# Two transformer-like layers on one core: row maxima of two head pairs joined and turned together, second score product eight slots behind instead of five

## The reference, cut to what matters

```python
xn = _layernorm(x)
q, k, v = split(xn @ qkv_w + qkv_b)          # 32 heads of 16 columns
q, k = _rope(q, cos, sin), _rope(k, cos, sin)
scores = einsum('bhqd,bkhd->bhqk', q, k) / 4 + causal mask
probs = softmax(scores)                       # needs each row's maximum first
ctx = einsum('bhqk,bkhd->bqhd', probs, v) @ out_w + out_b
g = silu(ffn(xn))                             # three products with 1376 hidden columns
x = x + ctx * g
```

## Time and profile before

| | us |
|---|---|
| median of three runs | 704.54 |
| lowest, highest | 700.82, 704.76 |
| profiled execution | 699.1 |
| its span | 697.4 |
| PE busy in the span | 622.3 (89%) |
| DVE, ACT, POOL busy | 395.2, 276.8, 370.6 |
| L932 + L941, both score products, PE busy | 44.7 + 37.4 |
| L918, turns of maxima, PE busy, 128 instructions | 19.2 |
| L1219, copies of turned maxima, ACT busy, 64 instructions | 37.4 |

### The profile page before, as it was taken

The page is one execution under the profiler, slowest core; times in us unless marked ns, Lnnn a source line. Parts: engine busy times, 40 slices in busy tenths (PEclk is TensorE's granted clock), DMA queues, the critical chain, the costliest instruction groups (busy, mean ns, idle before and its releaser), DMA issues. The chain is left out here.

```text
span 697.4 us, 9829 instructions
## 1 busy us (share of the span) xinstructions
PE 622.3 (89%) x3372; PEld 425.3 (61%) x3372; DVE 395.2 (57%) x973; ACT 276.8 (40%) x442; POOL 370.6 (53%) x541
## 2 busy tenths in 40 slices
PE   1987899999999997789999999999799999998992
PEld 1855565666557785555656655778577565756660
DVE  4849868666346581986876652649425151515035
ACT  2624545555534422246455564451212343132331
POOL 4765556544333745756554433449802987424445
PEclk9999999999999999999999999999999999999897
DMA  8486765554412326786484336434200000000003
GB/s 294 144 294 200 219 174 159 169 129 110 120 47 75 91 90 169 245 261 181 130 236 135 92 92 261 164 128 138 97 1 0 1 0 1 1 0 1 0 1 120
DMA packets 59889, 83.24 MB, mean 119 GB/s; under 512 B 17840, under 2 KB 26288, under 8 KB 59840
## 3 DMA queue, kind: packets, MB, share of 16 engines
q1 hardware_dynamic: 56192, 71.35, 34.6%
q10 hardware_dynamic: 3648, 11.27, 4.3%
HBM read 64.78 MB, written 26.99 MB: 132 GB/s over the span
## 5 line engine op out<-in xcount | busy, mean ns | idle before, releaser
L729 POOL TENSOR_TENSOR w_lo<-raw,w_hi 128x512 fp32r<-128x512 f32 x98 | 130.8, 1340 | 85.9 <-ACT w_hi L1250 81.5
L1433 DVE CUSTOM_DVE_ANT_0 score_ps<-score_ps,causal 128x512 f32<-128x512 f32 (+3 forms) x256 | 119.9, 517 | 57.3 <-PE score_ps L932 56.7
L1297 ACT ACTIVATE probs_T<-scoreT_ps 128x1024 f32<-128x1024 f32 (+1 forms) x96 | 84.8, 884 | 79.5 <-PE scoreT_ps L941 78.8
L904 PE MATMUL proj_ps<-xn_hi,w_hi 128*128 128x512 f32 x224 | 100.1, 447 | 4.4 <-POOL w_lo L729 2.4
L906 PE MATMUL proj_ps<-xn_lo,w_hi 128*128 128x512 f32 x224 | 88.6, 395 | 0.0
L905 PE MATMUL proj_ps<-xn_hi,w_lo 128*128 128x512 f32 x224 | 88.3, 394 | 0.0
L727 POOL TENSOR_SCALAR w_hi<-raw 128x512 fp32r<-128x512 f32 x50 | 31.1, 621 | 88.4 <-PE proj_ps L906 74.3
L932 PE MATMUL score_ps<-k_st,q_st 50*128 50x512 f32 (+3 forms) x256 | 44.7, 386 | 18.3 <-DVE row_max L1433 15.3
L904 PEld LDWEIGHTS proj_ps<-xn_hi,w_hi 128*128 128x128 f32 x224 | 42.1, 188 | 29.6 <-issue 12.1
L749 POOL TENSOR_SCALAR_AFFINE_SELECT probs_T<-probs_T 128x256 f32<-128x256 f32 x128 | 50.2, 416 | 17.0 <-ACT probs_T L1297 17.0
L932 PEld LDWEIGHTS score_ps<-k_st,q_st 50*128 50x128 f32 x256 | 21.8, 185 | 59.9 <-issue 30.2
(11 more groups left out here) (310 smaller groups left out, 1366.3 us busy)
## 6 DMA issues: line engine op xcount, KB each, us to landing
raw<-w SPq DMA_DIRECT2D x98, 256.0 KB, 2.7
rows<-rows_hi SPq DMA_DIRECT2D x32, 256.0 KB, 3.4
arranged<-tern SPq DMA_DIRECT2D x96, 85.0 KB
q_st<-rows SPq DMA_DIRECT2D x32, 200.0 KB
k_st<-rows SPq DMA_DIRECT2D x32, 200.0 KB
rows<-rows_lo SPq DMA_DIRECT2D x16, 256.0 KB, 4.0
gate_w<-arranged ACTq DMA_DIRECT2D x4, 704.0 KB, 7.0
up_w<-arranged ACTq DMA_DIRECT2D x4, 704.0 KB, 8.5
```

The lines of the kernel that those rows point to most:

```text
L729: nc.gpsimd.tensor_tensor(w_lo[n % SPLIT][:, :], raw[n % RAW][:, :], F32(w_hi[n % SPLIT][:, :]), ALU.subtract).then_inc(unit_ready, 1)
L904: nc.tensor.matmul(acc, lh, rh, start=first, stop=False)
L1297: nc.scalar.activation(probs_T[gp % 4][:, c:c + 2 * w].rearrange("p (h c) -> p h c", h=2), scoreT_ps[:, :, 0:w], ACT.Exp, scale=0.25).then ...
L1433: m = nc.vector.tensor_tensor_reduce(out=block, in0=block, in1=causal[:, S - w:], scale=1.0, scalar=-3e38, op0=ALU.add, op1=ALU.max, accum ...
```

## The change

The three tasks of both pairs of a group are collected before the maxima are joined: `join_maxima`, `max_turn` and `max_out` run once for a group (in slots 6, 12, ... 48) where they ran once for a pair (in slots 3, 6, ... 48). `max_cols` now holds 98 columns in one buffer, with the pairs at columns 0 and 64 and the heads 32 apart. LAG is 8 instead of 5, so SCORE_SLOTS is 56 instead of 53, and the V products, the turns of contexts and the reads of stacks move with it.

```diff
-LAG = 5
+LAG = 8
...
 def read_in(s):
-    return next((g for g in range(1, GROUPS) if (1 if g == 1 else max(6 * g - 6, unit_slot(K_UNIT[g // 2]) + 6)) == s), None)
+    return next((g for g in range(1, GROUPS) if (1 if g == 1 else max(6 * g - 4, unit_slot(K_UNIT[g // 2]) + 6)) == s), None)
...
 def max_in(s):
-    j = s // 3 - 1
-    return j if s % 3 == 0 and 0 <= j < PAIRS else None
+    g = s // 6 - 1
+    return g if s % 6 == 0 and 0 <= g < GROUPS else None
 
 def pv_in(s):
-    g, kt = divmod(s - 12, 6)
-    return (g, kt) if s >= 12 and g < GROUPS and kt <= NT else None
+    g, kt = divmod(s - 15, 6)
+    return (g, kt) if s >= 15 and g < GROUPS and kt <= NT else None
 
 def ctx_in(s):
-    return (s - 17) // 6 if s >= 17 and (s - 17) % 6 == 0 and (s - 17) // 6 < GROUPS else None
+    return (s - 20) // 6 if s >= 20 and (s - 20) % 6 == 0 and (s - 20) // 6 < GROUPS else None
...
-    max_cols = sb("max_cols", [P, 2, NT, 34], f32r)
+    max_cols = sb("max_cols", [P, NT, 98], f32r)
...
-            def max_turn(b, j):
-                pe.wait_ge(max_ready, PAIRS * b + j + 1)
-                n = use(b, ("max", j))
+            def max_turn(b, g):
+                pe.wait_ge(max_ready, GROUPS * b + g + 1)
+                n = use(b, ("max", g))
                 if TURN_BANK[n][1]:
                     pe.wait_ge(turn_done(n), TURN_BANK[n][1])
                 for qt in range(NT):
-                    m = nc.tensor.transpose(turn_bank(n)[0:34, qt * P:(qt + 1) * P], F32(max_cols[:, j % 2, qt, :]), ident[:, :])
+                    m = nc.tensor.transpose(turn_bank(n)[0:98, qt * P:(qt + 1) * P], F32(max_cols[:, qt, :]), ident[:, :])
...
-                        if x == 0:
-                            pe.wait_ge(*copied(b, ("max", j)))
+                        if x == 0 and j % 2 == 0:
+                            pe.wait_ge(*copied(b, ("max", j // 2)))
...
-                for hh in range(2):
-                    m = nc.scalar.activation(q_st[g % 3][64 * hh:64 * hh + 2, j % 2, :], turn_bank(n)[32 * hh:32 * hh + 2, :], ACT.Copy)
+                for p in range(2):
+                    for hh in range(2):
+                        r = 64 * p + 32 * hh
+                        m = nc.scalar.activation(q_st[(GROUPS * b + g) % 3][64 * hh:64 * hh + 2, p, :], turn_bank(n)[r:r + 2, :], ACT.Copy)
                 m.then_inc(turn_done(n), 1)
...
-                        if s % 3 == 2:
-                            join_maxima(b, s // 3)
+                        if s % 6 == 5:
+                            join_maxima(b, s // 6)
```

More of the change, by code:

```diff
@@ L323, in program @@
     causal = sb("causal", [P, S], f32)
-    row_max = sb("row_max", [P, 2, 8], f32)
+    row_max = sb("row_max", [P, 2, NT, 4], f32)
     stat = sb("stat", [P, NT, 6], f32)
@@ L797, in _ @@
                     if b == 0 and u == 1:
-                        nc.gpsimd.memset(F32(max_cols[:, :, :, :]), 0.0).then_inc(cols_set, 1)
+                        nc.gpsimd.memset(F32(max_cols[:, :, :]), 0.0).then_inc(cols_set, 1)
                 if b:
@@ L1212, in copy_out, with max_out @@
                 return nc.scalar.activation(dst, turn_bank(n)[:, :], ACT.Copy)
-            def max_out(b, j):
-                n, g = use(b, ("max", j)), GROUPS * b + j // 2
+            def max_out(b, g):
+                n = use(b, ("max", g))
                 act.wait_ge(turned, n + 1)
-                for hh in range(2):
-                    m = nc.scalar.activation(q_st[g % 3][64 * hh:64 * hh + 2, j % 2, :], turn_bank(n)[32 * hh:32 * hh + 2, :], ACT.Copy)
+                for p in range(2):
+                    for hh in range(2):
+                        r = 64 * p + 32 * hh
+                        m = nc.scalar.activation(q_st[(GROUPS * b + g) % 3][64 * hh:64 * hh + 2, p, :], turn_bank(n)[r:r + 2, :], ACT.Copy)
                 m.then_inc(turn_done(n), 1)
@@ L1433, in row_maxima, with join_maxima @@
                         m = nc.vector.tensor_tensor_reduce(out=block, in0=block, in1=causal[:, S - w:], scale=1.0, scalar=-3e38, op0=ALU.add,
-                                                           op1=ALU.max, accum_out=row_max[:, j % 2, 2 * qt + hh:2 * qt + hh + 1])
+                                                           op1=ALU.max, accum_out=row_max[:, j // 2 % 2, qt, 2 * (j % 2) + hh:2 * (j % 2) + hh + 1])
                 m.then_inc(part_ready, 1)
-            def join_maxima(b, j):
-                dve.wait_ge(part_ready, TASKS * b + 3 * j + 3)
-                if PAIRS * b + j == 0:
+            def join_maxima(b, g):
+                dve.wait_ge(part_ready, TASKS * b + 6 * g + 6)
+                if GROUPS * b + g == 0:
                     dve.wait_ge(cols_set, 1)
-                if PAIRS * b + j >= 2:
-                    b0, j0 = divmod(PAIRS * b + j - 2, PAIRS)
-                    dve.wait_ge(turned, use(b0, ("max", j0)) + 1)
-                maxima = row_max[:, j % 2, :].rearrange("p (t h) -> p t h", t=NT)
-                hi, lo = (max_cols[:, j % 2, :, x:34:32] for x in range(2))
+                else:
+                    b0, g0 = divmod(GROUPS * b + g - 1, GROUPS)
+                    dve.wait_ge(turned, use(b0, ("max", g0)) + 1)
+                maxima = row_max[:, g % 2, :, :]
+                hi, lo = (max_cols[:, :, x:98:32] for x in range(2))
                 nc.vector.tensor_copy(hi, maxima).then_inc(max_hi, 1)
-                dve.wait_ge(max_hi, PAIRS * b + j + 1)
+                dve.wait_ge(max_hi, GROUPS * b + g + 1)
                 nc.vector.tensor_tensor(lo, maxima, F32(hi), ALU.subtract).then_inc(max_ready, 1)
```

## The result

The changed kernel took 712.54 us in the median of four runs (710.22 to 718.04), the kernel before 704.65 (700.82 to 704.77) beside it: a ratio of 1.0145, with a 95% interval of 1.0103 to 1.0187; it is estimated from all their runs, the two medians alone give 1.0112. The forecast was 711 us.

What follows compares the result with a forecast made beforehand. DVE was taken to bound slots 0 to 13, PE the rest. Batch 0 +3.4 and batch 1 +3.1 made 699.1 + 6.5 = 705.6 us profiled; with the median 5.4 above, 711 us, 0.9% slower, range 701 to 718.

Steps and rivals of the forecast that it cites:

- ACT's four copies hold PE: Behind turns (start T), the exponential releases PE at T + 3.77 us; slots 20 to 50 wait, 4.4 us a batch.
- In the rest of the batch DVE has time: Outside the head, DVE has time, so the joins removed there were taken as worth nothing.
- DVE's waits gone behind slot 22: A sign of being right: new slot numbers part the rope steps from joins and contexts on DVE; no size given.
- Slots 14 to the last: From slot 14 to the last slot's start: 112.2 us against 107.28, +4.9 us, including 4.4 of ACT waits.
- Head: Slots 0 to 13, set by DVE, and slot 14's wait for ACT: -1.5 us in batch 0, -1.8 in batch 1.
- the late reads that I had noted as a bound: Batch 1, slot 12 already waited 1.09 us for a read; a wait was to stay, so -1.8 us was taken.
- reads from group 3 on: Issued four slots ahead of use, not six: between nothing and 1.09 us for each of ten reads, taken as nothing.
- Rival 2: Slower clock and late data in the longer-idling head: two further stretches, +2.8 us, median 714 us; chance 0.17.
- a clock below 1.00 in slots where it was full: One of the signs that would show the prediction wrong; the sum of 6.5 us held no term for it.
- Rival 3: Wider weight loads of the turns on PE not covered: upper bound 63 ns each, +4.0 us, median 715; chance 0.03.
- Rivals 1 and 4: Rival 1: ACT does not hold PE, median 698.8 us, chance 0.11; rival 4: half the ACT waits hidden, 705, 0.08.
- The turns saved: Eight turns a batch go from PE; two in the head give nothing, six give 0.44 us each, 2.6 a batch.

Runs made afterwards that it cites:

- turn first: The changed kernel with the turn of maxima ahead of the slot's fill on PE instead of behind it: 706.67 us, ratio 1.0067.
- The edit of the copies in the kernel before: The kernel before with two more ACT copies after each pair's own two, so four in a row behind each turn: 712.15 us, ratio 1.0142.
- turn first with early reads: The changed kernel with the turn ahead of the fill, copies ahead of the rope copy on ACT, and reads issued at other slots: 705.63 us, ratio 1.0041.
- the lag alone: The kernel before with LAG 8 instead of 5, joins, turns and copies still for each pair: 712.99 us, ratio 1.0132.
- the last comparison of the experiments: Changed kernel with turn ahead of fill, early reads, front-loaded fill, split copies (700.90 us, 0.9982), beside the kernel before with the same reads and fill (702.48 us, 1.0004).

## Why the prediction was right, and where not

**ACT's four copies hold PE: right.** The copies, the exponential and the release came at T + 3.79 against T + 3.77, in 13 of the 14 places forecast. In slots 26, 32, 38 and 44 the profile shows 0.28 to 0.30 us of wait. From the scores to the fill slot 32 takes 1.10 us (136.11 to 137.21), against 0.55 without a wait (138.41 to 138.96 in the kernel with turn first), so the cost is the forecast 0.55, half of which is not listed as a wait. The listed wait of slot 50 is 0.93 (forecast 1.0), that of slot 14 1.38 (1.7). Slots 20 and 38 were over-priced, because PE waited for DVE just ahead (0.43 and 0.67 us) and so came later to ACT, in slot 20 so late that no wait was left. The profile lists 7.5 us for the 14 waits where I had said 11 to 12; with a quarter of a us more for each, as in slot 32, an estimate of what they cost is 11. The edit of the copies in the kernel before shows the mechanism by itself; turn first takes it away.

**"In the rest of the batch DVE has time", and DVE's waits gone behind slot 22: wrong.** Behind the scores of slot 14 DVE still holds PE for 2.2 us in five places of batch 0 (slots 20, 24, 28, 33 and 38), against 1.7 in two places before. The new slot numbers parted the old meetings of slots 23 and 25 and made others: in slot 24 a rope step of 2.2 us on DVE stands ahead of the row maxima, and in slots 20 and 38 the gate product sits idle ahead of them, though its tanh stands ahead of the copies on ACT. Only in slot 33 (0.62 us) is it a tanh behind the copies, which I missed when I followed what stands behind them to the exponentials and the context copy.

**Slots 14 to the last: +4.9 forecast, +10.1 measured in batch 0.** Idle time gives +3.9 (5.88 against 1.95) where +2.9 stood in the sum. Busy time gives +6.2 (111.51 against 105.33) where I had +2.0 (107.3 of work). Of the 4.2 us between, the 6.58 us at the halved clock make 3.1 by the price above. The work itself was right: turn first with early reads ran this stretch at full clock and was busy 107.75 us. The last transposed product of batch 0 starts at 199.56 us, not near 196.

**Head: -1.5 and -1.8 forecast.** To the transposed product of slot 14 it is 39.58 us (44.55 to 84.13) against 40.5 before, -0.9, and -1.0 in batch 1 (43.28 against 44.27). In batch 1 the late reads that I had noted as a bound came: slots 0, 6 and 12 waited 0.52, 2.04 and 1.83 us for rows, in place of two waits of 2.8 us together. I had taken nothing for reads from group 3 on, and there none was late: those of groups 0, 1 and 2 were.

**Rival 2, the clock in the longer-idling head: it came on top of the forecast.** It had 0.17 and gave 714. Idle time in the heads rose from 6.8 and 8.9 to 8.6 and 11.1 us, less than the 4 us it counted, but slot time at the halved clock rose from 3.4 to 17.1 us. At 0.47 us each that is up to 6.4 us, half of the 12.9 by which the span grew (less where PE would have waited anyway). Against the kernel before's other executions, which spread by their own clock, it is less (below). The step that failed is therefore the choice to leave the clock at full in the sum, because batch 0 had shown none; a clock below 1.00 in slots where it was full was one of the prediction's own signs of being wrong.

**Rival 3, wider weight loads: wrong.** From the turn to the V step it is 0.53 us with 98 columns (132.99 to 133.52), as it was with 34. A load of 98 columns took 126 ns, 29 more than one of 34 and not the 63 of my upper bound. **Rivals 1 and 4**, no or half of the waits for ACT: wrong; the waits came at 13 of 14 places. Rival 1 was also priced wrongly: a release 0.4 us sooner would not have taken away waits of 1.7, 1.24 and 1.0 us.

**The turns saved, 2.6 us a batch: borne out, by one comparison of profiles.** With the lag at eight in both and at full clock, the part from slot 14 on is busy 110.59 us with a turn for each pair (the lag alone, batch 1) and 107.75 with one for each group (turn first with early reads, batch 0): 2.8 us less for six turns fewer. The order of turn and fill differs between the two as well. In the last comparison of the experiments PE is busy 4.4 us less with 16 turns fewer, 7.0 us by the forecast price of 0.44 each; the waits and the clock, which add busy time of their own, can't be parted from that.

**How near 711 us lies is in part luck.** In the profile the slots grew by 15.9 us and not 6.5, and the rest of the program came out 3.0 us shorter. The median of before that the forecast started from was high: over the 74 runs of the kernel before beside the experiments the mean is 702.2 us, and the changed kernel's four runs lie 11 us above it.

## What to carry to other kernels

Grouping small steps of one engine makes a burst on the next: four copies of 0.6 us in place of two held PE back although no engine had more work. Ask of a burst not only who waits for what stands right behind it, but who waits for each later step in that queue, and start the burst earlier (turn ahead of the fill) before shortening it. A longer lag takes work from the start of the pipeline, where another engine sets the pace and PE idles in part, to where PE sets it: 5.5 us more there against 1.7 us less at the start, in the batch whose later part ran at full clock.

## What the runs showed of the hardware

- The spread of runs of one kernel goes mostly with its TensorE clock. Put 2 x (1 - mean clock) x span as the time at 1.2 GHz. Of 74 runs of the kernel before, the 16 with under 31 us of it (mean 28.5) took 700.0 us in the mean, the 13 with over 41 (mean 43.9) took 704.4: 0.28 us of time for each us. A line through all 74 has 0.32 and leaves a deviation of 1.2 us, where the times themselves deviate by 2.1. So the price over the whole program is lower than 0.47; that this is because part of the halved time falls on waits is my reading.
- By this line the four runs of the changed kernel, with 42.0 us in the mean against 36.5, owe some 1.8 of their 11 us over all runs of before to the clock. The one profile, with its 12.9 us, overstates it. The kernel with doubled copies had only 32.0 us and lost its 10 us without the clock.
- A wait costs more than the profile lists. At 98.39 in the kernel with doubled copies 0.22 us are listed, and from the scores to the fill (97.78 to 98.81) it is 1.03 us against 0.55 without a wait: 0.48 us. The 1.7 us of busy time that seven more waits brought there are the same thing, 0.24 us for each. That PE's pipe has to fill again is my reading; the rows show only the distances.
